# Tiles 8, 10, 12 and 14 get their convolution from split operands in 256-column matmuls, with a changed order of work in their pairs

## The reference

```python
# layer 0
c = conv1d(x, weight, padding=4, groups=4)        # 9 taps, 64 -> 64 channels in 4 groups of 16
c = c + (cond @ c_weight.T)[:, :, None] + fside[None, :, None]
out = c @ W.T + b
scores = softmax(c @ gate_w.T + gate_b); pick the best of 4 ranks r in (8, 16, 32, 64)
x = x + out + (c @ A[:r].T @ B[:, :r].T)          # weighted by the normalised score (1)
# layer 1
c = einsum(agg_w(cond), x) + agg_b(cond)          # a 64 x 64 matrix for each sample
w = sparsemax(c @ W_router.T + b_router)
x = x + c @ W_base.T + b_base + (low-rank addition of 8 experts, weighted by w)
```

## Time and profile before

| | |
|---|---|
| median of three runs | 501.01 us |
| profiled execution | 503.35 us |
| its span, first to last instruction | 501.4 us |
| granted TensorE clock | 1.000 of full speed |
| PE / PEld / DVE / ACT / POOL busy | 495.5 / 459.9 / 355.2 / 132.8 / 147.0 us |
| convolution matmuls (L1330) | 512 instructions, 16 for each sample |

### The profile page before, as it was taken

How to read it: one execution, slowest core, us unless ns; L and a number is a source line. 1 busy time by engine, 2 the same in 40 slices (tenths; PEclk the granted TensorE clock), 3 DMA queues, 4 the chain that set the end, 5 groups by cost and what they waited for, 6 DMA issues and landing times.

```text
span 501.4 us, 8273 instructions
## 1 busy us (share of the span) xinstructions
PE 495.5 (99%) x2921; PEld 459.9 (92%) x2921; DVE 355.2 (71%) x827; ACT 132.8 (26%) x272; POOL 147.0 (29%) x124
## 2 busy tenths in 40 slices
PE   8999999999999999999899999999999999999997
PEld 7999999999999999999899989898998989899886
DVE  3966998857676886767789778586757658675654
ACT  3832244312332223331262321121112112111200
POOL 1000010004443142442205753250626226062520
PEclk9999999999999999999999999999999999999999
DMA  8934305428476475654999743433415233240312
GB/s 293 347 138 152 114 1 158 148 96 246 163 250 203 175 233 179 215 184 169 350 406 367 285 160 114 128 103 120 154 44 188 84 127 105 104 170 1 126 43 84
DMA packets 41124, 84.32 MB, mean 168 GB/s; under 512 B 3803, under 2 KB 16731, under 8 KB 41084
## 3 DMA queue, kind: packets, MB, share of 16 engines
q1 hardware_dynamic: 32028, 61.42, 36.6%
q10 hardware_dynamic: 9056, 22.38, 12.2%
HBM read 58.82 MB, written 24.97 MB: 167 GB/s over the span
## 4 chain that ended last, share of the span: by engine, by line
PE 89%; DMA 6%; DVE 2%; POOL 1%; issue 1%; SPq 1%; ACT 0%; DVEq 0%; ACTq 0%; POOLq 0%
PE b_p L1364 8%; PE b_x L1384 6%; PE b_x L1383 6%; PE b_x L1381 6%; PE b_m L1330 5%; PE b_p L1365 4%; PE b_y L1384 4%; PE b_y L1381 4%; PE b_y L1383 4%; PE b_m L1340 3%; PE b_z L1383 2%; PE b_z L1384 2%; PE b_z L1381 2%; PE b_y L1330 2%; PE b_w L1384 2%; PE b_w L1383 2%
## 5 line engine op out<-in xcount | busy, mean ns | idle before, releaser
L600 ACT CAST a_hi<-mixed 128x512 fp32r<-128x512 f32 x63 | 38.1, 620 | 158.7 <-DVE mixed L911 80.4
L1364 PE MATMUL b_p<-wp,a_hi 128*128 128x464 f32 (+1 forms) x224 | 72.6, 377 | 0.0
L542 POOL TENSOR_TENSOR xs<-xs,mixw_sb 128x512 f32<-128x512 f32 x28 | 36.0, 1298 | 116.8 <-DMA xs<-x_scratch 70.8
L923 DVE TENSOR_TENSOR s_lo<-mixed,s_hi 128x512 fp32r<-128x512 f32 x56 | 44.0, 815 | 27.4 <-ACT s_hi L612 27.4
L1365 PE MATMUL b_p<-wp,a_lo 128*128 128x232 f32 (+1 forms) x224 | 60.2, 269 | 0.0
L612 ACT CAST s_hi<-mixed 128x512 fp32r<-128x512 f32 x56 | 34.7, 620 | 86.5 <-POOL mixed L514 50.4
L916 DVE TENSOR_TENSOR a_lo<-mixed,a_hi 128x512 fp32r<-128x512 f32 x63 | 44.5, 732 | 9.3 <-ACT a_hi L600 8.8
L514 POOL TENSOR_TENSOR mixed<-mixed 128x512 f32<-128x512 f32 x13 | 16.8, 1289 | 107.9 <-DVE a_lo L916 107.9
L1364 PEld LDWEIGHTS b_p<-wp,a_hi 128*128 128x128 f32 x224 | 42.1, 188 | 5.1
L1365 PEld LDWEIGHTS b_p<-wp,a_lo 128*128 128x128 f32 x224 | 42.8, 191 | 0.6
L1381 PE MATMUL b_y<-wb_hi,s_hi 128*128 128x464 f32 (+2 forms) x112 | 41.5, 370 | 0.0
(11 more groups left out here) (273 smaller groups left out, 1211.8 us busy)
## 6 DMA issues: line engine op xcount, KB each, us to landing
blk<-x_scratch SPq DMA_DIRECT2D x16, 512.0 KB, 4.1
xs<-in_x SPq DMA_DIRECT2D x30, 256.0 KB, 3.2
x_scratch<-xs SPq DMA_DIRECT2D x30, 256.0 KB, 5.2
blk<-in_xblk SPq DMA_DIRECT2D x14, 516.0 KB, 4.3
xs<-x_scratch SPq DMA_DIRECT2D x28, 256.0 KB, 3.1
out_dram<-xs SPq DMA_DIRECT2D x27, 256.0 KB, 2.1
w_raw<-in_wcat SPq DMA_DIRECT2D x8, 546.0 KB, 9.3
praw<-in_wcat ACTq DMA_DIRECT2D x8, 464.0 KB, 6.3
```

Of the source, the lines that this page charges most:

```text
L542: pool.tensor_tensor(x_rows, x_rows, bbase[:, a:b], ALU.add).then_inc(x_biased[q], 1)
L600: act.copy(a_hi[:, op, :, :], mixed[:, op, :, :]).then_inc(ahi_done[op], 1)
L923: dve.tensor_tensor(s_lo[:, i, :, :], mixed[:, S_AT[i], :, :], hi(s_hi[:, i, :, :]), ALU.subtract).then_inc(slo_done[i], 1)
L1364: pe.matmul(both, x_hi, wp[:, k, :, 0:PLAIN[l]], start=(k == 0), stop=False, skip_group_check=True)
```

## The change

For tiles T = 8, 10, 12, 14 (`shifted(T)`: the even tile a of pairs 3 to 6) the convolution is done on unpadded blocks. One block (8 positions x 16 channels) is multiplied by the taps for 16 output positions, 256 columns: the 4 before it, its own 8 and the 4 behind it. The own 8 are the middle half of a PSUM bank. The outer parts belong to the neighbouring blocks, on the partitions above and below: ACT copies them out (`take_z`), four DMAs move them by one partition (`move_z`), and GpSimd adds them to `mixed` (`add_z`). The operands are split as in the dense layer, so each block takes three matmuls. The lines of the other tiles' convolution are not changed.

```diff
+            def shift_step(T, n, gp):
+                pe.wait_ge(shift_lo, 2 + sample(T, n) + 1)
+                for gl in range(2):
+                    at = QB * (2 * gp + gl)
+                    x_hi, x_lo = xh[:, n, at:at + QB], blk_lo[T % 2][:, BANK * n + at:BANK * n + at + QB]
+                    dst = shift_bank(gp)[:, :].rearrange("p (a c) -> p a c", c=2 * GC)[:, :, GC * gl:GC * (gl + 1)]
...
+                    pe.matmul(dst, x_hi, w_hi, start=True, stop=False)
+                    pe.matmul(dst, x_hi, w_lo, start=False, stop=False)
+                    ins = pe.matmul(dst, x_lo, w_hi, start=False, stop=True)
+                ins.then_inc(mix_done, 1)
```

PE's order in pairs 3 to 6 (after plain(t1) and plain(t2)); `emptied` waits for ACT's copy out of the bank:

```diff
+                shift_step(a, 0, 0)
+                pe.wait_ge(fin12, g)
+                shift_step(a, 0, 1)
+                pe.wait_ge(fin22, g)
+                product_a(g, P1, b_x, A11, B11)
+                emptied(a, 0, 0)
+                shift_step(a, 1, 0)
+                emptied(a, 0, 1)
+                shift_step(a, 1, 1)
...
+                product_a(g, P2, b_z, A12, B21)
+                turn_pair(g)
...
+                product_a(g, P4, b_w, A22, T4)
+                emptied(a, 1, 1)
+                product_s(g, P5, b_y, S1, T1)
```

DVE's order in pairs 3 to 6 (semaphores of the waits cut):

```diff
+                gate_scores(g)
+                sum_shift(a, 0, 0)
+                sum_shift(a, 0, 1)
+                split_s(S1, g)
+                gate_weights(g)
+                split_s(S3, g)
+                sum_shift(a, 1, 0)
+                sum_shift(a, 1, 1)
+                split_s(S2, g)
+                split_ut(2 * g)
+                split_ut(2 * g + 1)
+                take_first(g)
...
+                take(b_y, 3, g, took_p5)
+                sum_mix(b, 0)
...
+                take(b_z, 0, g, fin11, BANK)
+                prep_split(0, g)
+                prep_split(1, g)
...
+                take(b_x, 1, g, took_u2)
...
+                take_plain(0, g)
+                split_s(S4, g)
+                sum_mix(b, 1)
+                prep_split(3, g)
+                prep_split(2, g)
+                split_a(A11, g + 1)
...
+                take(b_w, 2, g, took_w, BANK)
...
+                take(b_x, 2, g, fin21)
+                split_a(A12, g + 1)
+                split_a(A21, g + 1)
+                split_a(A22, g + 1)
+                take_plain(1, g)
...
+                take(b_x, 3, g, fin22, BANK)
...
+                take(b_y, 1, g, fin12, BANK)
+                if shifted(a + 2):
+                    low_x(a + 2, 0)
+                    low_x(a + 2, 1)
```

The moved parts, on SP and on GpSimd (`add_z` stands behind `prep` in GpSimd's order):

```diff
+                sp.dma_start(dst[1:EDGE + 1, 0, :], src[0:EDGE, 1, :]).then_inc(z_landed[n], 16)
+                sp.dma_start(dst[0:EDGE, 1, :], src[1:EDGE + 1, 0, :]).then_inc(z_landed[n], 16)
+                sp.dma_start(dst[EDGE + 1:P, 0, :], src[EDGE:P - 1, 1, :]).then_inc(z_landed[n], 16)
+                sp.dma_start(dst[EDGE:P - 1, 1, :], src[EDGE + 1:P, 0, :]).then_inc(z_landed[n], 16)
...
+                pool.wait_ge(z_landed[n], 32 * (T - SHIFTED) + 64)
+                pool.tensor_tensor(dst, dst, z_moved[n].rearrange("p v (a c) -> p v a c", c=CH),
+                                   ALU.add).then_inc(z_added, 1)
```

- GpSimd's sums are written to a place of their own, where the low parts are kept, and no longer into `mixed`. They wait for the product that read the low part before (P5, P7, P6, P3 of the pair before) and for `sum_mix`, and no longer for `split_a`:

```diff
-                pool.wait_ge(alo_done[A21], g + 1)
-                pool.wait_ge(alo_done[A22], g + 1)
-                pool.tensor_tensor(mixed[:, A22, :, :], mixed[:, A21, :, :], mixed[:, A22, :, :], ALU.add).then_inc(s_sum, 1)
...
+                pool.wait_ge(p_done[P5], users)
+                pool.wait_ge(sum_done, steps(2 * g + 2))
...
+                pool.tensor_tensor(s_raw(S1), mixed[:, A21, :, :], mixed[:, A22, :, :], ALU.add).then_inc(s_sum, 1)
```

```diff
                     for b in (0, 1, 3, 2):
                         prep_split(b, g)
-                if g == PAIRS - 1:
-                    split_plain()
                 dve.wait_ge(p_done[P5], made(g))
                 take(b_y, 3, g, took_p5)
...
                     take(b_x, 1, g, took_u2)
                 if g == PAIRS - 1:
+                    split_plain()
                     split_slot(B11, 0)
                     split_slot(B11, 1)
```

- SP loads the matrices of layer 1's first pair in the middle of pair 6, ahead of its stores and loads there, and not at its end:

```diff
+                    sp.wait_ge(mix_done, steps(a + 1))
+                    if g == PAIRS - 2:
+                        sp.wait_ge(agg_stored, 16)
+                        load_agg(PAIRS)
+                    load_blocks(a + 2)
```

More of the change, by code:

```diff
@@ L88, with shifted, steps, build @@
 AGG_PAIR, PREP_FIRST, PREP_LAST = 2, 3, 6
+SHIFTED = 8
+EDGE = P - 16
 def layer(g):
     return g // PAIRS
-def build(nc, x, xblk, front, wcat0, bcat0, bias0, wcat1, bcat1, b_base, pack, mixw, bias_k, out):
+def shifted(T):
+    return SHIFTED <= T < TILES and T % 2 == 0
+def steps(T):
+    return 2 * T + 2 * max(0, (min(T, TILES) - SHIFTED + 1) // 2)
+def build(nc, x, xblk, xwhole, front, wcat0, bcat0, bias0, wcat1, bcat1, b_base, pack, mixw, bias_k, out):
     x_t = x.rearrange("(t n) c h -> t (n c) h", n=2)
@@ L182, in build @@
         prep_hi = sb("prep_hi", [P, 4, HMAX], F32R)
+        kernels_end = sb("kernels_end", [P, TILES * P - 4 * HMAX])
+        taps_lo01 = sb("taps_lo01", [P, HALF_TAPS], F32R)
+        taps_hi = sb("taps_hi", [P, 2, HALF_TAPS], F32R)
+        with nc.sbuf_tensor("att_diag", [P, OQ, TILES], F32) as att_diag:
+            pass
+        taps_lo2 = sb("taps_lo2", [P, 2 * P], F32R)
+        taps_lo = [taps_lo01[:, 0:2 * P], taps_lo01[:, 2 * P:], taps_lo2[:, :], taps_lo3[:, :]]
+        z_moved = [halves[:, :, HALF_TAPS:HALF_TAPS + BANK // 2], z_moved1[:, :, :]]
+        z_out = [part[:, A21, :, :].rearrange("p k c -> p (k c)").rearrange("p (v c) -> p v c", v=2)
+                 for part in (a_hi_place, a_lo_place)]
         xs_turn = [part[:, T2, :, :].rearrange("p k c -> p (k c)")[:, 0:D] for part in (wb_rows, wb_raw)]
@@ L313, in made, with sample, shift_bank @@
             return g - FULL + 1
+        def sample(T, n):
+            return T - SHIFTED + n
+        def shift_bank(half):
+            return (b_m, b_y)[half]
         def a_free(eng, op, g):
@@ L594, in split_a @@
                 T = 2 * g + op // 2
-                if layer(g) == 0:
-                    act.wait_ge(sum_done, 2 * T + 2)
+                if shifted(T):
+                    act.wait_ge(z_added, sample(T, 1) + 1)
+                elif shifted(T - 1):
+                    act.wait_ge(z_added, sample(T - 1, 1) + 1)
+                    act.wait_ge(sum_done, steps(T) + 2)
+                elif layer(g) == 0:
+                    act.wait_ge(sum_done, steps(T) + 2)
                 else:
-                    act.wait_ge(sum_done, 2 * T + 1 + op % 2)
+                    act.wait_ge(sum_done, steps(T) + 1 + op % 2)
                 a_free(act, op, g)
                 act.copy(a_hi[:, op, :, :], mixed[:, op, :, :]).then_inc(ahi_done[op], 1)
-            S_AT = {S1: A22, S2: A11, S3: A21, S4: A12}
             S_USER = {S1: P5, S2: P6, S3: P7, S4: P3}
@@ L758, in _ @@
                     split_s(S2, g)
-                gate_exp(2 * g)
+                if not together(2 * g):
+                    gate_exp(2 * g)
                 if g > FULL:
@@ L1209, in _ @@
+            for g in range(FULL, LAST + 1):
+                if shifted(2 * g + 2):
+                    shift_pair(g)
+                    continue
+                if not together(2 * g):
+                    gate(2 * g)
                 if g == PAIRS:
@@ L1215, in _ @@
                     split_s(S4, g)
-                gate(2 * g + 1)
+                if together(2 * g):
+                    gate_scores(g)
+                    gate_weights(g)
+                else:
+                    gate(2 * g + 1)
                 if g == FULL:
@@ L1584, in _ @@
                 if g == AGG_PAIR:
-                    pe.wait_ge(sum_done, 2 * (t2 + 1))
+                    pe.wait_ge(sum_done, steps(t2 + 1))
                     aggregate(0)
+                if shifted(t1 + 2):
+                    shift_pair(g)
+                    continue
                 if g == FULL:
```

422 lines of the change are left out of this document (336 added, 86 removed).

## The result

The changed kernel takes 505.64 us (median of 6 runs, 503.84 to 507.15) where the kernel before takes 501.27 (6 runs, 500.93 to 502.67): ratio 1.0078, 95% interval 1.0058 to 1.0098. The forecast was 499.0 with a range up to 501.7: wrong in its sign.

The account below looks back on a forecast made before the run. The prediction took PE's own instruction sequence to bound the kernel (89% of the span). Its terms, -3.0 - 1.5 + 1.5 + 1.0 = -2.0 us, took the median from 501.01 to 499.0, range 496.3 to 501.7.

Parts of the forecast that it names:

- PE's work, -3.0: Convolution in pairs 3 to 6: twelve 256-column matmuls at 0.1175 us replace 1.78 us a sample, saving 3.0 us.
- rival C: Shifted convolution: output in 16 runs of 16 slows each matmul to 0.2125 us, +6.1 for -3.0, total 508.1; chance 0.09.
- The wait for layer 1's matrices, -1.5: Start of layer 1 after P1: issuing the matrix load some 20 us earlier removes PE's 1.48 us wait; bounds -1.5 and 0.
- DVE in pair 7, +1.5: Pair 7: split_plain behind P6's take has no cover, so PE's lora into b_x waits 1.5 us; bounds 0 and 2.2.
- DVE at the end of pairs 3 to 6, +1.0: DVE splits beside GpSimd sums delay P7's take and take_plain, costing 1.0 us over four pairs; bounds 0 and +4.8.
- D: Pairs 3 to 6: all six DVE splits run beside GpSimd sums, takes 1.2 us late each, 502.8; chance 0.14, whole or part.
- Counted at nothing: Effects in the shifted pairs and layer 1, such as joint gates, moved parts and layer 1's S1 split, credited with no time.
- The bank waits: New PE waits between shift steps (a,0,0) and (a,1,0), covered by other work: zero cost, bounds 0 and 0.5 a pair.
- the moved parts: Copy, four DMAs and GpSimd addition, wanted by the next pair's plain(t1) some 17 us after the copy: no cost.
- the low parts for the next tile: Two DVE splits of 1.3 to 2.6 us, wanted 5.1 us into the pair: tight, but counted at nothing.
- Layer 1, no pair changes: Layer 1: S1's split stands behind the takes, where nothing of PE waits, so no pair's length changes.
- The chance of "faster": Probability given to the changed kernel beating the kernel before: 0.70, against 0.12 for same and 0.18 for slower.

Follow-up runs that it names:

- both_orders: Changed kernel with pair 7's split_plain and pairs 3 to 6's preparation splits earlier, layer 1's sums before the x addition, take_plain before A12, A21, A22: 498.40 us, ratio 0.9940.
- sums_late: Changed kernel, but in pairs 3 to 6 GpSimd's sums wait for DVE's last plain take of the pair: 499.56 us, ratio 0.9963.
- agg_early: Kernel before with only the load of layer 1's first matrices issued early in pair 6: 501.24 us, ratio 0.9995.
- plain_early: Changed kernel with pair 7's split_plain back at its old place on ACT and DVE: 504.75 us, ratio 1.0067.
- after: First profile of the changed kernel, unaltered; its comparison measured 505.64 us, ratio 1.0078 to the kernel before.
- again: Changed kernel, unaltered, compared and profiled a second time: 504.33 us, ratio 1.0055 to the kernel before.
- before_c: Kernel before the change, unaltered, in its third profile: 501.55 us.
- before_b: Kernel before the change, unaltered, in its second profile: 500.90 us.
- prep_early: Changed kernel with all four DVE preparation splits before P6's take in pairs 3 to 6: 502.45 us, ratio 1.0016.

## Why the prediction was wrong

**PE's work, -3.0: right.** Pairs 3 to 6 take 122.96 before and 120.06 where nothing waits (`both_orders`, `sums_late`): -2.90. The step is 0.120 in a tile's first sample and 0.117 in its second (0.1175 predicted). So rival C (0.2125) is refuted, and with it what the prediction cites for it, as far as runs of 16 go: they cost nothing that can be seen.

**The wait for layer 1's matrices, -1.5: the mechanism right, the size wrong.** The load is early and the wait gone (issued 13 us sooner against the start of pair 7, not 20), but it was worth 1.48 in one execution, 0.41 and 0 in two others, and 0.2 by the medians of `agg_early`, which is within the noise. I had the bound 0 and a hint: the profiled execution stood 2.3 above the median of the runs, and I took that as an even offset. A wait that ends on a transfer, while the DMA engines are full, is the first thing that can differ between that execution and the median.

**DVE in pair 7, +1.5: right.** PE waits 1.47 there, released by P7's take. But it is not a cost that stands alone: taken away while the sums of pair 9 stand behind a load, it comes back as 2.11 in pair 9 (`plain_early`); with the sums ahead of that load it is a gain.

**DVE at the end of pairs 3 to 6, +1.0: this is the step that failed, and the term that decided.** It is 124.77 - 120.06 = +4.7, at its bound of +4.8, and a shifted pair is 31.19 long, the number that the prediction gave for D (31.2). I saw the mechanism and its price (1.29 for 0.60, 3.06 for 1.28; here three splits lose 2.2). The row of 3.06 was misread in one thing: what GpSimd did beside it was `prep` (160.23 and 161.51, 128x464), not a sum, but it too is GpSimd work on operands in SBUF. The count was wrong: I let two of three splits meet a sum, since GpSimd must itself wait for P7, and left 0.25 us a pair over. All three meet one. The first sum in fact waits for nothing but the last `sum_mix`, which DVE's splits follow at once; the first two lose 1.1 beside it, and that brings A11's split (234.25) to the moment at which P7's end lets the second sum go (234.20). The wait that I counted as protection lasts 0.37. The take comes 2.2 late against a slack of 1.2, so PE waits 1.08, and the pair is 1.18 longer.

The rows fit work in turns, not at half speed: A11's split, started 0.05 behind a sum, ends when that sum (235.45) and 0.6 us of its own are past, and the next sum, started at 235.45 behind the split's own turn, takes 1.74 in place of 1.29.
The Trainium skill has this in "SBUF — State Buffer", section "Who interferes with whom": a DVE instruction with two inputs in SBUF contends with a GpSimd instruction that reads SBUF, the later one being blocked, and one with at most one input in SBUF, outside the two-port modes, does not contend. The rows after agree on both (1.72 for 0.60 from start to start; the take of b_w 0.68).

**Counted at nothing.** The bank waits, the moved parts and the low parts for the next tile: right, PE waits nowhere in the first half of a shifted pair. "Layer 1, no pair changes": wrong, though in few us. The changed kernel makes S1's split wait for the third sum in place of the first, and pairs 8 to 10 take 88.46 to 90.75 in `after`, `again` and `plain_early`, against 88.36 before. That varies between executions, as it hangs on the landing of a load.

**The sum with measured terms.** Pair 2 to the end: 413.6 to 414.1 (`before_c`, `before_b`), -2.9 convolution, +4.7 splits, +1.6 or +1.1 for pair 7 (28.73 against 27.16 and 27.65), +0.1 to +0.2 pairs 8 to 10, which is 417.1: +3.0 to +3.6, as `after` and `again` show (417.05, 417.15). `again` measured +2.9. The first comparison measured +4.4; which part of the 1.5 us between the two is pair 9's wait (pairs 8 to 10 are up to 2.4 longer in a profile) stays open.

Rival D was the right one. Even so it would have said 502.8, since it took the -1.5 as well; without that it says 504.3. Of its two waits only the one for P7's take is seen in the changed kernel; the one for `take_plain` appears once the first is gone (`prep_early`). The chance of "faster" adds up to 0.69, not 0.70, which changes nothing.

## What to carry over

When a change lets an engine start earlier, ask whether it reads SBUF at the same time as the engine that sets the end, and lay both out in time, instruction by instruction: here the sums, freed from the splits they used to wait for, ran into them, and a wait put back on GpSimd (`sums_late`) or the changed orders of `both_orders` (498.40) turned +0.55% into -0.4% and -0.6%. Credit a removed wait that ends on a transfer only after the profiled execution has been held against the median, and by more than one profile if the two differ. A wait removed upstream of a chain bound by transfers can come back at the next thing that waits for a load.

## What the runs showed of the hardware

A DVE split with both inputs in SBUF takes 0.60 from start to start alone (`sums_late`) and 1.72 beside GpSimd additions that read SBUF (`after`); one of these goes from 1.29 to 1.74. A DVE addition with one operand in PSUM is not slowed (0.68). A float32r matmul of 256 columns starts 0.117 to 0.120 after the last one when its output lies in 16 runs of 16, and 0.1175 when it lies in one run of 256. After a wait of PE the next step is longer as well, 0.34 for 0.23 in `after`. One load of 128 KB between full queues was 1.48 late in one profile of a kernel, and 0.41 and 0 in two others of the same kernel.
